# A sequence mixer and a gated MLP in one kernel: another order of the first block on VectorE and ScalarE, and weight parts that land singly

## What is computed

```python
x = x + mixer(layernorm(x))                  # first stage
x = x + mlp(layernorm(x))                    # second stage

def mixer(h):                                # per sequence, 64 heads of 16, state 128
    z, xBC, dt = split(h @ W_in * mup)       # 1024, 1280 and 64 columns
    xBC = silu(conv_b + sum(conv_w[:, k] * shifted(xBC, k) for k in range(4)))
    x, B, C = split(xBC)                     # 1024, 128, 128
    dt = softplus(dt + dt_bias)
    dA = exp(-dt * exp(A_log))
    for t in range(L):
        state = state * dA[t] + (dt[t] * x[t]) outer B[t]
        y[t] = state @ C[t]
    y = y + D * x
    g = y * silu(z)
    return (g * rsqrt(mean(g * g) + eps) * norm_w) @ W_out

def mlp(h):                                  # inner width 1408, weights are -1, 0 or 1
    return ((silu(h @ gate_w.T * gate_s) * (h @ up_w.T * up_s)) @ down_w.T) * down_s
```

## Time and profile before

| what | value |
|---|---|
| median of three runs | 766.48 us |
| lowest, highest | 765.35, 768.88 us |
| the profiled execution | 770.17 us |
| its span, first to last instruction | 768.5 us |
| PE busy | 735.6 us, 96% |
| DVE busy | 513.3 us, 67% |
| ACT busy | 492.6 us, 64% |
| POOL busy | 292.2 us, 38% |

### The profile page before, as it was taken

The page is one execution under the profiler, slowest core; times in us unless marked ns, Lnnn a source line. Parts: engine busy times, 40 slices in busy tenths (PEclk is TensorE's granted clock), DMA queues, the critical chain, the costliest instruction groups (busy, mean ns, idle before and its releaser), DMA issues.

```text
span 768.5 us, 20313 instructions
## 1 busy us (share of the span) xinstructions
PE 735.6 (96%) x8486; PEld 609.4 (79%) x8486; DVE 513.3 (67%) x845; ACT 492.6 (64%) x933; POOL 292.2 (38%) x235
## 2 busy tenths in 40 slices
PE   4878999999999999999999998989999999999997
PEld 4866778888887887887887886778888888888886
DVE  5977876987987897797797796763624532632331
ACT  6998978978978978979879878624312321321330
POOL 2055276366456547637617707630021011002002
PEclk9988999999999999999999999999999999999999
DMA  9831444484485286366376389535122013002002
GB/s 296 241 93 28 95 112 112 99 243 126 85 243 139 81 210 170 84 160 202 84 210 191 81 227 312 189 99 163 42 70 96 0 42 123 0 16 94 0 1 85
DMA packets 42300, 94.97 MB, mean 124 GB/s; under 512 B 9889, under 2 KB 15777, under 8 KB 42017
## 3 DMA queue, kind: packets, MB, share of 16 engines
q1 hardware_dynamic: 42208, 93.67, 42.8%
HBM read 84.73 MB, written 17.57 MB: 133 GB/s over the span
## 4 chain that ended last, share of the span: by engine, by line
PE 84%; ACT 8%; DVE 4%; issue 2%; DMA 1%; POOL 0%; SPq 0%; ACTq 0%; DVEq 0%; POOLq 0%
PE ps_y L1742 10%; PE ps_proj L1729 10%; PE ps_proj L1271 8%; PE ps_proj L1272 8%; PE ps_proj L1273 8%; PE ps_out L1729 6%; PE ps_x L1729 6%; PE ps_y L1347 5%; PE ps_x L1358 4%; PE ps_out L1371 4%; PE ps_out L1372 3%; PE ps_out L1373 3%; PE ps_x L1324 3%; ACT ring L721 2%; ACT ring L725 2%
## 5 line engine op out<-in xcount | busy, mean ns | idle before, releaser
L532 POOL TENSOR_TENSOR ring<-tokd,ring 128x1024 f32<-128x1024 f32 x64 | 122.3, 1926 | 175.7 <-ACT tokd L716 130.9
L1271 PE MATMUL ps_proj<-xn_hi,win_x_hi 128*128 128x256 f32 x352 | 104.6, 297 | 4.8 <-ACT cin L667 2.9
L1272 PE MATMUL ps_proj<-xn_lo,win_x_hi 128*128 128x256 f32 x352 | 100.2, 285 | 0.0
L1273 PE MATMUL ps_proj<-xn_hi,win_x_lo 128*128 128x256 f32 x352 | 99.9, 284 | 0.0
L962 DVE SCALAR_TENSOR_TENSOR cx<-cin,consts,cx 128x256 f32<-128x256 f32 x240 | 96.3, 477 | 0.0
L1017 DVE TENSOR_TENSOR ring<-ring,ps_tok 128x1024 f32<-128x1024 f32 x64 | 76.0, 1216 | 14.1 <-ACT ring L725 14.0
L1598 POOL TENSOR_TENSOR res<-res,hidden 128x512 f32<-128x512 f32 (+1 forms) x16 | 20.1, 1258 | 166.3 <-DVE hidden L1661 165.3
L1271 PEld LDWEIGHTS ps_proj<-xn_hi,win_x_hi 128*128 128x128 f32 x352 | 67.6, 192 | 18.0 <-issue 8.3
L1271 PE MATMUL ps_proj<-xn_hi,win_z_hi 128*128 128x256 f32 x256 | 74.6, 291 | 0.2 <-ACT sz L664 0.2
L1272 PE MATMUL ps_proj<-xn_lo,win_z_hi 128*128 128x256 f32 x256 | 72.8, 284 | 0.0
L1273 PE MATMUL ps_proj<-xn_hi,win_z_lo 128*128 128x256 f32 x256 | 72.6, 284 | 0.0
(11 more groups left out here) (186 smaller groups left out, 1876.9 us busy)
## 6 DMA issues: line engine op xcount, KB each, us to landing
ring<-cum_dram SPq DMA_DIRECT2D x128, 256.0 KB, 4.8
xin<-x SPq DMA_DIRECT2D x8, 512.0 KB, 3.9
res<-x SPq DMA_DIRECT2D x32, 128.0 KB, 2.8
x_dram<-res SPq DMA_DIRECT2D x32, 128.0 KB, 2.4
res<-x_dram SPq DMA_DIRECT2D x16, 256.0 KB, 2.6
out<-res SPq DMA_DIRECT2D x15, 256.0 KB, 2.0
x_in_sb<-x_dram SPq DMA_DIRECT2D x3, 1024.0 KB, 5.6
gate_w_copy<-gate_w SPq DMA_DIRECT2D x4, 704.0 KB, 6.4
```

What stands on the lines that cost most here:

```text
L532: pool.tensor_tensor(ring[:, g, :, :], own, ring[:, g, :, :], ALU.subtract).then_inc(diffed, 1)
L1271: pe.matmul(out, hi[:, k, :], xn_hi[:, k, :], start=(k == 0), stop=False)
L1272: pe.matmul(out, hi[:, k, :], xn_lo[:, k, :], start=False, stop=False)
L1273: made = pe.matmul(out, lo[:, k, :], xn_hi[:, k, :], start=False, stop=(k == KT - 1))
```

## The change

Two independent parts. In the first block, on ScalarE: `weight_hi` of pieces 11 and 12 go behind `make_skip(0, 0)`, `evacuate(1, 1)` goes ahead of the clamps of step 1, and `weight_hi` of piece 13 goes behind the last `fade` of step 1. On VectorE: `norm_stats(1)` and `normalise(1)` go up between the first `mix` calls, and `weight_lo` of pieces 11 and 12 go ahead of `make_xpad(0, 1)`. The wait on `lo_made` ahead of `update_state(0, 0)` is for an instruction of VectorE's own that stands ahead of it.

On SP: a weight part waits for the part just before it (one in flight), and parts 4 and 5 go behind the tables g = 0 and 1 of step 15.

```diff
             def load_weights(n):
 
-                if n >= 2:
-                    sp.wait_ge(hand.weights_in[n % 2], 16 * (n // 2))
+                if n >= 1:
+                    sp.wait_ge(hand.weights_in[(n - 1) % 2], 16 * ((n + 1) // 2))
...
                         sp.dma_start(xin[:], hand.x1_by_block[0, :, 0:2, :]).then_inc(hand.first_in, 16)
-                        load_weights(4)
-                        load_weights(5)
...
                 for g in range(GROUPS):
                     load_cums(i, 1, g)
+                    if last and g == 1:
+                        load_weights(4)
+                        load_weights(5)
...
                 weight_hi(EVENTS)
                 evacuate(0, 8)
-                weight_hi(EVENTS + 1)
                 evacuate(0, 9)
...
                 make_skip(0, 0)
+                weight_hi(EVENTS + 1)
+                weight_hi(EVENTS + 2)
                 evacuate(1, 0)
                 gate_hi(0)
                 keep_tok(1)
+                evacuate(1, 1)
                 clamp(1, 0)
                 clamp(1, 1)
-                weight_hi(EVENTS + 2)
...
                     square(c - 1)
-                    evacuate(i + 1, 1)
+                    if not first:
+                        evacuate(i + 1, 1)
                     clamp(c, 2)
                 fade(c, 1)
                 if not last:
                     evacuate(i + 1, 2)
-                if first:
-                    weight_hi(EVENTS + 3)
                 clamp(c, 3)
                 fade(c, 2)
                 fade(c, 3)
+                if first:
+                    weight_hi(EVENTS + 3)
...
                 mask_cb(0)
+                norm_stats(1)
                 mix(0, 0)
                 mix(0, 1)
                 weight_lo(EVENTS - 1)
                 mix(0, 2)
+                normalise(1)
                 mix(0, 3)
-                norm_stats(1)
+                dve.wait_ge(lo_made, EVENTS)
                 update_state(0, 0)
-                normalise(1)
                 weight_lo(EVENTS)
...
                 gate(0, 0)
+                weight_lo(EVENTS + 1)
+                weight_lo(EVENTS + 2)
                 make_xpad(0, 1)
-                weight_lo(EVENTS + 1)
                 gate_lo(0)
-                weight_lo(EVENTS + 2)
```

## The result

The changed kernel takes 771.35 us (769.18 to 773.70), the kernel before 766.99 us beside it. The ratio is 1.0058, 95% interval 1.0039 to 1.0077. The prediction was 762.3 us, with 758.9 to 765.2 as its range: wrong in sign. The profiled execution of the changed kernel took 772.79 us, its span 771.0.

The account below looks back on a forecast made before the run. TensorE was taken as saturated from 120 us to the last block, ScalarE as the bound up to about 80 us. First block 3.6 plus last block 0.6 gave 4.2 us off the 766.48 us median: 762.3 us, range 758.9 to 765.2.

Parts of the forecast that it names:

- ScalarE's four terms: First block: moving pieces 11 to 13 ends step 1's fades earlier by 0.6 + 1.3 + 0.6 + 1.3 = 3.8 us.
- Behind it the low part of piece 13 and `soft` start at 78.7: First block, VectorE: the work behind step 1's last mix starts at 78.7 instead of 82.45 us.
- together about 2.7 of low parts, so they just fit: First block, VectorE: low parts of pieces 11 and 12 fit into its 2.79 us idle ahead of `xpad`.
- Does TensorE keep it?: First block: TensorE waits 3.3 us for the state near 88 us; a clock fall costs 0 to 1.7, taken as 0.2.
- rival C: TensorE gives back 1.7 us, by the clock after its 88 us wait or a later last-block fetch; 764.4 us, chance 0.22.
- The last block, 0.6 us: Last block: TensorE's 3.57 us instruction stall stays near no change, bounded by 5.3 us won and 2.0 lost; 0.6 won.
- rival B: Last block: single parts bring instructions 2 us sooner, the stall halves and the clock stays up; 759.4 us, chance 0.17.
- Tables g = 2 and 3: hidden: Last block, SP: step 15's tables stand behind part 5, which waits for part 4, at no cost.
- The last ones wait for TensorE to free their groups: Last block, SP: the eight table loads last 14.49 us, to 489.03, since the last wait for TensorE, so delay is hidden.
- part 4 lands some 5 us after: Last block, SP: part 5 waits for part 4, landing some 5 us after 477 us.
- `xin`: hidden, 3 us to spare: Last block: `xin` lands near 478 us and VectorE reads it at 481.27, so its delay costs nothing.
- Rival E: SP's queue behind part 7 brings the residual rows 4.7 us too late for `make_x1`; 767.6 us, chance 0.04.

Follow-up runs that it names:

- e10: e7 with GpSimd's `make_xw` and state fade moved ahead of `fold_squares` in step 1 of the first block; 764.31 us, 0.9950 of the kernel before.
- e6: e1 with VectorE's low part of piece 13 moved behind the first half of step 1's state; 1.0059 of the kernel before.
- e1: The changed kernel with SyncE's queue as in the kernel before, so only the first block's new order; 766.62 us, 0.9985 of the kernel before.
- before again: The kernel before, unchanged, run once more; 766.70 us.
- e11: The changed kernel with parts 4 and 5 behind all four groups of tables, still one in flight; 768.37 us, 1.0002 of the kernel before.
- e5: The changed kernel with parts 4 and 5 back at the head of the last body, still one in flight; 774.45 us, 1.0086 of the kernel before.
- e3: The changed kernel with part 5 alone moved behind all four groups of tables, one in flight; 769.58 us, 1.0012 of the kernel before.
- e4: The changed kernel with two parts in flight again, parts 4 and 5 still behind g = 1; 767.16 us, 0.9994 of the kernel before.
- e7: The changed kernel with two parts in flight and parts 4 and 5 behind all four groups of tables; 764.86 us, 0.9966 of the kernel before.
- e8: e7 with VectorE's low part of piece 13 moved behind the first half of step 1's state; 1.0061 of the kernel before.
- e2: The kernel before with only SyncE's part of the change, first block in the old order; 773.80 us, 1.0089 of the kernel before.

## Why the prediction was wrong, step by step

**ScalarE's four terms were right.** `evacuate(1, 0)` came 0.4 us earlier (0.6 said), the squares' wait went, and the last mixes end at 77.62 (77.4 said): 3.6 of 3.8 us.

**"Behind it the low part of piece 13 and `soft` start at 78.7"** failed by 1.5 us for `soft`, 1.35 of them in the low part, and "together about 2.7 of low parts, so they just fit" by 1.9. I took 1.33 to 1.42 us per piece from a trace in which the low parts of pieces 11 to 13 met no GpSimd operation. Moved to where ScalarE made room, they met one each in the changed kernel's trace. e10 shows it.

**"Does TensorE keep it?": mis-sized.** The wait was 4.29 and not 3.3 us, since VectorE was late and TensorE was not; the half clock lasted 6.8 us where 3.4 was assumed. Its first 1.4 us fell into the wait and cost nothing; from this `update` to the next z projection TensorE took 7.63 us and not 5.38 as before, so 2.3 us were lost, not 1.7. This is rival C's event. Waits that went absorbed most of it, as the step assumed. Of ScalarE's 3.6 us some 1.8 were left on TensorE (the carries); VectorE's 1.35 taken off, that leaves about 0.4 for this term, which I had at 0.2.

**"The last block, 0.6 us": the wrong baseline.** The stall which I bounded was 3.57 us in one execution and 1.06 in another of the same program. In all traces it was 1.06 to 3.57 (with e6's 2.89) where parts go two at a time at the head of the body, and 0.1 to 1.19 in the other arrangements. The instruction queue does account for its length: in all 14 traces TensorE runs dry 6.93 us after its carry of step 14 starts, and goes on 1.2 to 1.6 us after the next 16 KB packet of queue q8 has landed. That packet starts 7.96 us after the carry in the trace of before, 6.72 and 7.32 in e1 and e6, 4.94 in before again, and 4.85 to 5.86 in the rest. So the change may shorten the stall by letting the packet start sooner, but the ranges touch, and what part of it is chance stays open. Either way rival B's event, the stall halved, did occur, and its 759.4 did not come.

**"Tables g = 2 and 3: hidden"** is the step that decided. It put the cost at nothing, and the last block took 51.7 us where the two traces of before took 46.3 and 44.3. These 5.4 to 7.4 us, less the 1.8 won in the first block, enclose the 4.4 us between the medians. Two things in it were wrong. "The last ones wait for TensorE to free their groups" took the times of before, 485.8 to 489, for the need; these were late themselves because TensorE had lost 3.6 us at 475. Freed of that, TensorE frees group 2 at 479.9, and the tables were issued 4.9 us after that. And "part 4 lands some 5 us after" its issue took the landing of a lone part, when `xin` and four table loads left within 4 us ahead of it: it took 8.96. GpSimd waited 6.45 us, and the RMS scale stood behind it. The prediction compared times of issue and never asked what is queued behind a waiting `diff`. The table of runs shows the price: one in flight costs 1.0, 0.64 and 0.36% in the three places, with intervals that just overlap in the last.

**"`xin`: hidden, 3 us to spare"** failed the same way: 481.27 was late by the stall. It cost 0.71 us here and 3.43 on VectorE in e11.

**Rival E** pointed at the right edit, SyncE parked at a part, but at the wrong place: part 7 and the residual rows, when it was part 5 and the tables. That the chance of slower was put at 0.04 comes from treating each parked load apart, and each against slack read in one trace.

## What to carry to other kernels

A wait added to a queue that only issues DMAs is paid by everything behind it: list the loads behind it with the time at which their readers will want them in the new kernel, not the time in a trace which has the very stall that the change removes. With one bulk part in flight, putting it behind the small loads that the critical chain needs took back 0.8% here (e5 to e11). With two in flight the place made no difference clear of noise, and two in flight had the lower ratio in all three places. When an operation of VectorE with both inputs in SBUF is moved, look at what GpSimd runs in its new place.

## What was unexpected in the hardware

- VectorE's 0.74 us subtraction took 2.10 and 2.39 us beside a GpSimd operation, and mixes of 1.22 us with one input in PSUM took their usual time beside it. When VectorE was first, in the kernel before at 56.09, it was GpSimd's `diff` that took longer, 2.27 us for 1.91.
- Around one wait of the first block, TensorE's half clock grew with the wait: none with 1.07 to 1.31 us (the four traces with the old order, near 91 us), 3.4 us with 2.90 (e10), 6.8 us with 4.3 (the changed kernel, e1, e3, e4, e5, e7, e11), 10.2 us with 7.17 and 7.43 (e6, e8). The length of the wait does not settle it: in the last block it was 3.4 us with the changed kernel's 5.83, and 6.8 us with e2's 3.21. It can begin before the wait ends, in the changed kernel at 88.45 us for a wait that ends at 89.81.
- The same eight parts landed in 3.9 to 9.0 us in the changed kernel, 4.0 to 7.7 in e7 and 4.8 to 10.4 in e4; the longest, 8.96 in the changed kernel and 10.36 in e4, had table loads beside them.
- From the MLP's first matmul to its last, every trace has 249.59 us; from there to the end of the span it is 3.1 to 5.2 us, and for the kernel before 4.4 in one execution and 3.1 in the other.
